# The first steps of a grouped-query attention stage: norms, banks, scalings and weight casts moved between steps

## The reference

```python
x = x + attn_a(layernorm(x))     # 32 heads of 16, rotary angles, causal
x = x + ffn(layernorm(x))        # x W + b, and the two best of 8 low-rank experts
x = x + attn_b(layernorm(x))     # 32 query heads on 8 key heads of 128
x = x + ffn(layernorm(x))        # the same weights as the second

def attn_b(x):
    q, k, v = x @ Wq.T, x @ Wk.T, x @ Wv.T        # 4096, 1024 and 1024 columns
    q, k = rmsnorm(q, q_norm_w), rmsnorm(k, k_norm_w)     # per head of 128
    s = q @ k.T / sqrt(128) + slope[head] * (key - query) # causal
    return (softmax(s) @ v) @ Wo.T                # four query heads share one key head
```

## Time and profile before

| | us |
|---|---|
| median of 3 runs | 1619.59 |
| lowest, highest | 1617.97, 1619.84 |
| the profiled execution | 1617.08 |
| its span, first to last instruction | 1615.3 |

### The profile page before, as it was taken

How to read it: one execution, slowest core, us unless ns; L and a number is a source line. 1 busy time by engine, 2 the same in 40 slices (tenths; PEclk the granted TensorE clock), 3 DMA queues, 4 the chain that set the end, 5 groups by cost and what they waited for, 6 DMA issues and landing times.

```text
span 1615.3 us, 25452 instructions
## 1 busy us (share of the span) xinstructions
PE 1511.1 (94%) x8968; PEld 1172.3 (73%) x8968; DVE 1115.7 (69%) x2866; ACT 816.0 (51%) x2115; POOL 417.9 (26%) x407
## 2 busy tenths in 40 slices
PE   3998999998897899999999999999999999999997
PEld 2863444443786788888888888888888888888776
DVE  5668777770665677677677677677767767767873
ACT  3523555566333455555555555556555555555531
POOL 4102000010543131331322223143133132224333
PEclk9997999999998999999999999999999999999999
DMA  4363443301200010100100000011010010001000
GB/s 149 97 139 54 54 59 49 41 2 56 64 8 24 17 27 1 40 27 1 40 8 19 14 28 27 1 40 27 1 40 27 1 40 7 20 6 35 1 20 33
DMA packets 40207, 54.28 MB, mean 34 GB/s; under 512 B 5776, under 2 KB 21392, under 8 KB 40080
## 3 DMA queue, kind: packets, MB, share of 16 engines
q1 hardware_dynamic: 40080, 52.65, 13.7%
HBM read 44.04 MB, written 8.39 MB: 32 GB/s over the span
## 4 chain that ended last, share of the span: by engine, by line
PE 59%; DVE 5%; issue 5%; ACT 4%; POOL 2%; ACTq 0%; DVEq 0%; POOLq 0%
PE ps L50 17%; PE ps L52 17%; PE ps L51 16%; PE ps L1520 6%; PE ps L1495 2%; DVE ab_qt_l L1772 1%; ACT ab_w_h L1626 1%; ACT ab_squares L1657 1%; DVE ab_pt_l L1780 1%; ACT prob L1645 1%; POOL ab_o_l L1416 1%; PE ps L241 1%; ACT ab_pt_h L1673 0%; PE ps L1497 0%; ACT ab_kt_h L1666 0%
## 5 line engine op out<-in xcount | busy, mean ns | idle before, releaser
L1645 ACT ACTIVATE prob<-prob,ab_neg_max 128x128 f32<-128x128 f32 (+7 forms) x256 | 201.1, 786 | 250.3 <-DVE ab_neg_max L1763 249.2
L1780 DVE TENSOR_TENSOR ab_pt_l<-ps,ab_pt_h 128x512 fp32r<-128x512 f32 x288 | 198.1, 688 | 79.4 <-ACT ab_pt_h L1673 78.5
L1673 ACT CAST ab_pt_h<-ps 128x512 fp32r<-128x512 f32 x288 | 172.1, 598 | 122.3 <-PE ps L1520 121.8
L1763 DVE CUSTOM_DVE_ANT_0 prob<-ps,rel 128x512 f32<-128x512 f32 (+3 forms) x256 | 146.0, 570 | 102.4 <-PE ps L52 101.5
L50 PE MATMUL ps<-ab_w_h,ab_xt_h 128*128 128x512 f32 (+1 forms) x512 | 186.3, 364 | 6.8 <-DVE ab_v_l L1800 6.6
L1041 DVE TENSOR_REDUCE ra_part_max<-ps 128x1 f32<-128x512 f32 (+3 forms) x318 | 156.5, 552 | 47.8 <-PE ps L943 28.7
L1520 PE MATMUL ps<-ident,prob 128*128 128x128 f32 x1152 | 173.4, 273 | 4.6 <-DVE ab_qt_l L1772 3.3
L1788 DVE TENSOR_SCALAR prob<-prob,ab_recip 128x128 f32<-128x128 f32 (+7 forms) x256 | 169.3, 661 | 9.1
L52 PE MATMUL ps<-ab_w_h,ab_xt_l 128*128 128x512 f32 (+1 forms) x512 | 174.1, 340 | 0.0
L51 PE MATMUL ps<-ab_w_l,ab_xt_h 128*128 128x512 f32 (+1 forms) x512 | 173.5, 339 | 0.0
L1405 POOL TENSOR_TENSOR ab_rms<-ab_ms_eps,neg_half 128x5 f32<-128x5 f32 x64 | 76.2, 1191 | 311.5 <-DVE ab_ms_eps L1805 310.6
(11 more groups left out here) (231 smaller groups left out, 3482.6 us busy)
## 6 DMA issues: line engine op xcount, KB each, us to landing
f_raw<-in_wqkv SPq DMA_DIRECT2D x32, 384.0 KB, 3.7
f_raw<-in_wbo SPq DMA_DIRECT2D x32, 256.0 KB, 2.6
ra_first_rows<-parts SPq DMA_DIRECT2D x36, 128.0 KB, 7.1
parts<-pa_stage SPq DMA_DIRECT2D x12, 256.0 KB, 2.9
parts<-f_raw SPq DMA_DIRECT2D x12, 256.0 KB, 3.4
ra_q_st<-parts SPq DMA_DIRECT2D x24, 128.0 KB, 6.0
ra_k_st<-parts SPq DMA_DIRECT2D x24, 128.0 KB, 6.6
f_raw<-in_wf SPq DMA_DIRECT2D x8, 324.0 KB, 3.3
```

Of the source, the lines that this page charges most:

```text
L1645: act.activation(prob[:, t % 2, h, 0:w], prob[:, t % 2, h, 0:w], ACT.Exp, bias=neg_max[:, t % 2, h, pieces_per_head(t % NT) - 1:pieces_per ...
L1673: act.copy(pt_h[:, n % PT, :], ring_bank("p", u, j)).then_inc(pt_high, 1)
L1763: dve.tensor_tensor_reduce(out=prob[:, t % 2, h, k0:k1], in0=ps[:, n % 2, a:b], in1=const["rel"][:, SLIDE - i * P + k0:SLIDE - i * P + k1] ...
L1780: dve.tensor_tensor(pt_l[:, n % PT, :], ring_bank("p", u, j), pt_h[:, n % PT, :].bitcast(F32), ALU.subtract).then_inc(emptied, 1)
```

## The change

Four things move; no instruction is added or left out.

- `shared_jobs`: step t may use the first max(1, t + 1) shared banks instead of max(1, t).
- `DEFERRED` becomes 3: squares, mean, power and scaling of tiles 3 and 4 stand in slots 4 to 6 of steps 1 and 2.
- `invert` and `centre` of the last norm for tiles 5, 6 and 7 stand in slot 1 of GpSimd's and slot 3 of VectorE's step -1, 0 and 1, behind the moments of the same step.
- For the first group alone, the `Wo` pieces are cast by ScalarE in slots 4 to 7 of step 0, and their low parts are made by GpSimd in slots 0 to 3 of step 1.

```diff
--- before.py
+++ after.py
@@ -1138,7 +1138,7 @@
         if t <= 1 and job[0] == "k":
             bank = first_keys
         else:
-            bank = min(banks[:max(1, t)], key=lambda b: last.get(b, -1))
+            bank = min(banks[:max(1, t + 1)], key=lambda b: last.get(b, -1))
         place[job] = n, bank, last.get(bank)
         last[bank] = n
 
@@ -1200,7 +1200,7 @@
     job_of = shared_jobs(SHARED, MIXED)
 
 
-    EARLY, DEFERRED, TAIL = 2, 5, 5
+    EARLY, DEFERRED, TAIL = 2, 3, 5
     with ExitStack() as own:
         def sb(name, shape, dt=F32):
             return own.enter_context(nc.sbuf_tensor(f"ab_{name}", shape, dt))
@@ -1407,6 +1407,8 @@
 
             def step(t):
                 for s in range(B_SLOTS):
+                    if s == 1 and TAIL <= t + LEAD - 2 < NT:
+                        b_norm.invert(pool, t + LEAD - 2)
                     if s == 4 and 0 <= t - 2 < B_STEPS:
                         pool.wait_ge(o_out, t - 1)
                         if t >= 3:
@@ -1420,7 +1422,7 @@
                     if s == 5 and DEFERRED <= t + 2 < B_STEPS:
                         invert_rms(t + 2)
                     g, i = divmod(t, NT)
-                    if i == 2 and s < KC and 0 <= g < KVB:
+                    if i == (2 if g else 1) and s < KC and 0 <= g < KVB:
                         split_low(2 * KC * g + KC + s)
                     if i == 5 and 3 <= s < 3 + KC and g + 1 < KVB and t >= 0:
                         split_low(2 * KC * (g + 1) + s - 3)
@@ -1434,7 +1436,7 @@
                 v, b, c = tiles(m, 0, 2, 3)
                 if 3 <= m <= 5:
                     split_low((0, 1, 3)[m - 3])
-                if c is not None:
+                if c is not None and c < TAIL:
                     b_norm.invert(pool, c)
                 if m == 4:
                     split_low(2)
@@ -1694,13 +1696,14 @@
                     if s == 4 and DEFERRED <= t + 2 < B_STEPS:
                         squares_of(t + 2)
                     g, i = divmod(t, NT)
-                    if i == 1 and s == 7 and 0 <= g < KVB:
-                        if g:
-                            act.wait_ge(out_done, NT * g)
+                    if i == 1 and s == 7 and 1 <= g < KVB:
+                        act.wait_ge(out_done, NT * g)
                         split_high_of(2 * KC * g + KC)
                         split_high_of(2 * KC * g + KC + 1)
-                    if i == 2 and s < 2 and 0 <= g < KVB:
+                    if i == 2 and s < 2 and 1 <= g < KVB:
                         split_high_of(2 * KC * g + KC + 2 + s)
+                    if i == 0 and s >= KC and g == 0:
+                        split_high_of(2 * KC * g + s)
                     if i == 5 and 2 <= s < 2 + KC and g + 1 < KVB and t >= 0:
                         act.wait_ge(projected, KC * (t + 2) + s - 1)
                         split_high_of(2 * KC * (g + 1) + s - 2)
@@ -1848,6 +1851,8 @@
                         qk_low_of(t + 1)
                     if turned_in(t, s):
                         pt_low_of(*turned_in(t, s))
+                    if s == 3 and TAIL <= t + LEAD - 2 < NT:
+                        b_norm.centre(dve, t + LEAD - 2)
                     if s in (2, 4, 6) and 0 <= t < B_STEPS:
                         normalise(t, s // 2 - 1)
                     if t == 0 and s == 2:
```

## The result

| | before | after |
|---|---|---|
| median of 4 runs each, us | 1618.78 | 1607.06 |
| lowest, highest | 1617.37, 1619.84 | 1605.24, 1609.68 |
| profiled execution, its span | 1617.08, 1615.3 | 1607.22, 1605.2 |

The changed kernel is faster: the ratio is 0.9929, with a 95% interval of 0.9912 to 0.9947. The medians are 11.7 us apart; -11.4 and 1608 were predicted. The 1608 was reckoned from 1619.6, the median of the first three runs of the kernel before; from the 1618.8 of all four the same -11.4 would give 1607.4.

A forecast was written before the change was run, and what follows sets the result against it. Bound taken: TensorE's 14.4 us of waits in the slices of 485 to 565 us, plus the lower clock behind some. The terms summed to -11.4 us, from the 1619.6 median to 1608.2, said as 1608; range 1604 to 1613.

The forecast's parts named there:

- Tile 5's norm costs: Centring tile 5 ahead of feed-forward tile 6's ranking delays the gating TensorE waits for: +1.2 us, bounds 0 to +1.3.
- The 2.37 doesn't go: Wait at the turn of norm tile 6: gains only 0.3 us, still behind ScalarE's cast; bounds -1.5 to +0.8.
- Bank waits: Waits of 1.66 us ahead of p(0,0) and p(1,0) go, 0.2 stays ahead of p(1,1): -1.66 and -1.45.
- Turn of tile 7: Wait ahead of the turn of norm tile 7 goes: -1.87 us, bounds 0 to -1.87.
- Scaling of tile 3: Ahead of tile 4's projection, a 4.07 us chain leaves 1.7 of the 3.22 wait: -1.5, bounds 0 to -3.2.
- Scaling of tile 4: The 2.58 us wait ahead of tile 5's projection goes, with its low clock (1.5); bounds 0 to -4.1.
- Clock: Less 1.2 GHz time: -1.5 us behind tile 5's projection wait, -1.7 (two thirds of 2.4) behind tile 4's.
- Rival (b): No wait long enough to lower the clock is left, at 502 either: -13.7 us, 1606; chance 15%.
- The weights: GpSimd's four subtractions in step 1 may hold up VectorE's first scaling and the centring: 0, bounds 0 to +2.3.
- Rival (c): Slower: new bank pairing makes the 1152 turns cost more; break-even 10 ns each, 1631 at 20 ns; chance 3%.
- (a): Freed waits return because tile 3's or 4's scaling is later than TensorE: -5 us, 1614.6; chance 12%.
- (d): A later step bound by its own time, such as a weight load, takes the gain back: 1619; chance 3%.

The follow-up runs named there:

- both bank runs: The bank edit alone on the kernel before, 1615.4 us; and the change with its bank edit undone, 1608.5 us.
- one of the later versions (1.58): The change with tile 5's last norm alone inverted and centred in the middle again, behind the ranking: 1606.1 us.

## Why the prediction was right, point by point

- **Where the time is.** Right: the stretch holds all of it. Its waits fell by 8.45 and the rest of it, nearly all of it clock, by 3.61; the sum had 8.2 and 3.2.
- **Tile 5's norm costs.** Right in mechanism and nearly in size: +0.95 for +1.2. I read the ranking's start as 1.2 late; it was 1.2 late (484.70 against 487.79, less 1.89), but GpSimd's first gating instruction was 0.24 shorter (0.40 instead of 0.64) after its longer idle. The run that undid it gave 0.96 back in that wait.
- **The 2.37 doesn't go.** Right: -0.45 for -0.3, with ScalarE's cast ahead of it as said. I didn't see that VectorE's mean square stood next in line with a collision of its own, which is why undoing the casts gave 0.3 to 0.4 and not 1.
- **Bank waits.** Right: 1.66 and 1.66 gone and 0.24 new ahead of p(1,1) (it starts 0.36 behind the row before it, instead of 0.12). Confirmed by both bank runs, -3.3 and +3.5 in waits. The 0.23 ahead of the projection of tile 3 stands nowhere in the sum.
- **Turn of tile 7.** Right, -1.78 for -1.87.
- **Scaling of tile 3.** The chain of 4.07 was right, the wait of 1.7 came out at 2.13. The collision that I bounded by 0 to +2.3 and took at 0 happened, once: 1.12 instead of 0.35. It held the mean square until 514.39, 0.7 behind the squares' end (513.68). This term was mis-sized for a reason that stood in the trace of before: three of the four subtractions come behind the inversion of tile 7, which started at 507.06 there, so they last until 507.06 + 0.5 + 3.8 = 511.4, not 510.5, and VectorE's work of that moment falls into them. Of the two operations named it caught one, the scaling; the centring behind it took 0.53.
- **Scaling of tile 4.** Right, the 2.58 gone.
- **Clock.** The total was right, the places weren't. I kept the low stretch behind 502 and let two thirds of that behind the projection of tile 4 go. Measured, the first went (the -2.82 at p(0,0) is -1.66 for the bank, +0.23 for the new wait, and some -1.4 for the clock) and the second stayed, shorter, for -1.1. That the two came to the same total was luck: the sum put the gain at the wrong place, and the same wait of 1.59 lowered the clock in one of the later versions (1.58) and not in this one. Rival (b) was thus half true.
- **The weights.** Charged with nothing beyond the casts; in truth this part brought nothing that can be seen, and put ScalarE's cast and GpSimd's collision on the path. The run without it has a stretch 0.72 shorter.
- Rival (c), a price of the new bank order, is refuted by the 173.4 us. Rivals (a) and (d) did not occur.

## What to carry to other kernels

Where a wait names one releaser, ask what that engine does next for the same waiter: the 2.37 us named one instruction and had two behind it, and a third showed when the second was moved. An operation that is moved forward in an in-order queue holds up what stood there if its own input isn't ready; tile 5's centring lost 0.95 us so, while the same move for tile 7 won 1.8. Work for GpSimd that "fits into idle time" is to be laid where VectorE has none of the operations named below on the path, and where the two start within a few hundredths of a microsecond the order is best made explicit with a wait.

## What the runs showed of the hardware

- **Collision of VectorE and GpSimd.** On VectorE a scaling of 128x256 from SBUF to SBUF took 0.35 us alone and 0.53, 1.12, 1.13, 1.46 and 1.50 beside GpSimd's subtractions of 1.3 us (0.80 beside the cast of 0.61); a centring of 128x512 took 0.53 to 0.55 alone and 1.19 and 1.44; a `SCALAR_TENSOR_TENSOR` of 128x5 with two inputs in SBUF took 0.16 to 0.17 alone and 0.84 beside a bias add. The last surprised me, as it moves next to nothing. What such a collision cost was what was left of GpSimd's instruction: the scalings of 0.53, 0.80, 1.12 and 1.13 ended 0.14 to 0.16 us behind the end of it (513.21 against 513.06 in the change), both mean squares of 0.84 ended 0.02 behind it. Of the three scalings that started 0.05 us ahead of GpSimd by the profile, one was not held up (0.35) and two were (0.80, 1.46). The Trainium skill (SBUF — State Buffer, "Who interferes with whom") says that VectorE contends with GpSimd also where an instruction has two SBUF inputs, against a GpSimd operation that reads SBUF; the 0.84 agrees. VectorE's operations with one input in PSUM, such as those that write `ab_nat` and `ab_v_l`, kept their times beside GpSimd (0.68 to 0.69 and 0.28).
- **The clock behind a wait.** It fell with each wait of 2.58 us or more in the stretch (2.58, 3.03, 3.22, 4.25, 4.51), and with none of 1.03 us or less that stood alone. Between, both were seen: it fell with 1.58, 1.92, 1.99, 2.13, 2.36 and 2.37, and with 1.21 with a 0.97 just ahead of it, and stayed up behind 1.21, 1.59, 1.66, 1.87, 1.90, 1.92, 1.98 and 2.36. So for waits of 1.2 to 2.4 us the wait alone doesn't tell, in these profiles, and by the rests in the table some 1.2 to 1.9 us hung on it each time. What else decides is left open here. A comparison of two schedules by one profile each should take the waits and the clock apart.
